# Fourteen products of ones, read by nothing, ahead of the first products of a graph network kernel

## What is computed

```
h = relu(layernorm(x))
for each of three layers:
    p   = relu(h @ Wp.T + bp)
    agg = segment_sum(p[src], dst) / max(count(dst), 1)
    h   = agg @ Wl.T + bl + h @ Wr.T
    after the first and the second layer: h = layernorm(relu(h)) * g + be
out = x + h
```

## Time and profile before

| | us |
|---|---|
| median of three runs | 1517.86 (1517.79 to 1518.0) |
| profiled execution, its own time | 1517.14 |
| span of that execution, first to last instruction | 1515.0 |
| PE busy in it | 1492.6 (99%) |
| DVE, ACT, POOL busy | 981.2, 687.1, 578.6 |

### The profile page before, as it was taken

One profiled execution on the slowest core, in us unless ns is written; L12 is line 12 of the kernel. 1 busy time (PEld: TensorE's weight loads), 2 busy tenths in 40 slices (PEclk: granted clock), 3 DMA queues, 4 the chain that ended last, 5 costly groups with the idle time before them and its releaser, 6 DMA issues.

```text
span 1515.0 us, 21400 instructions
## 1 busy us (share of the span) xinstructions
PE 1492.6 (99%) x7295; PEld 1221.5 (81%) x7295; DVE 981.2 (65%) x2164; ACT 687.1 (45%) x1267; POOL 578.6 (38%) x534
## 2 busy tenths in 40 slices
PE   7999999999999999999999999999999999999997
PEld 5787887888888888888888888888888888888886
DVE  7999975655555687777565655557766666555552
ACT  5545452232233577767322323357676652322322
POOL 4737754344323100100434442323354366444323
PEclk9999999999999999999999999999999999999999
DMA  8897877555554878887645555489999986455434
GB/s 301 319 377 249 271 249 238 111 90 89 93 85 56 242 263 306 271 275 253 216 108 90 88 93 88 54 244 320 345 329 324 328 292 207 80 89 90 73 45 60
DMA packets 152855, 291.72 MB, mean 193 GB/s; under 512 B 19885, under 2 KB 19948, under 8 KB 152620
## 3 DMA queue, kind: packets, MB, share of 16 engines
q1 hardware_dynamic: 123708, 224.81, 43.3%
q0 software_dynamic: 28464, 64.51, 24.7%
q10 hardware_dynamic: 576, 1.05, 0.2%
HBM read 132.33 MB, written 157.92 MB: 192 GB/s over the span
## 4 chain that ended last, share of the span: by engine, by line
PE 89%; DMA 4%; DVE 3%; issue 2%; POOL 1%; ACT 1%; SPq 0%; POOLq 0%; ACTq 0%; DVEq 0%
PE bank L737 12%; PE bank L736 12%; PE bank L738 12%; PE bank L724 9%; PE bank L820 7%; PE bank L822 7%; PE bank L821 7%; PE bank L841 7%; PE bank L843 7%; PE bank L842 7%; DMA node_x<-xn 2%; DVE stats L1073 1%; DVE rows_out L1103 1%; DVE h_low L1047 1%; DMA rows_in<-node_x,sorted_src 1%
## 5 line engine op out<-in xcount | busy, mean ns | idle before, releaser
L736 PE MATMUL bank<-w_high,h_low 128*128 128x512 f32 x900 | 374.6, 416 | 0.0
L737 PE MATMUL bank<-w_low,h_high 128*128 128x512 f32 x900 | 356.3, 396 | 0.0
L738 PE MATMUL bank<-w_high,h_high 128*128 128x512 f32 x900 | 354.5, 394 | 0.0
L981 ACT ACTIVATE h_high<-h_pre 128x500 fp32r<-128x500 f32 x120 | 74.6, 622 | 449.0 <-DVE h_pre L1284 449.0
L594 POOL DMA_INDIRECT rows_in<-node_x,sorted_src x120 | 124.1, 1034 | 274.6 <-PE bank L724 199.8
L927 ACT ACTIVATE h_high<-bank 128x512 fp32r<-128x512 f32 x221 | 131.4, 595 | 155.2 <-PE bank L724 155.0
L738 PEld LDWEIGHTS bank<-w_high,h_high 128*128 128x128 f32 x900 | 169.3, 188 | 40.3
L1050 DVE TENSOR_TENSOR h_low<-bank,h_high 128x512 fp32r<-128x512 f32 x152 | 105.0, 692 | 146.4 <-ACT h_high L927 144.5
L961 ACT ACTIVATE xn<-rows_in,off,rstd 128x512 f32<-128x512 f32 x237 | 189.4, 806 | 13.6 <-issue 9.0
L820 PE MATMUL bank<-xt_low,w_high 128*128 128x500 f32 x480 | 194.5, 405 | 0.0
L736 PEld LDWEIGHTS bank<-w_high,h_low 128*128 128x128 f32 x900 | 169.8, 189 | 30.3
(11 more groups left out here) (127 smaller groups left out, 2209.1 us busy)
## 6 DMA issues: line engine op xcount, KB each, us to landing
node_x<-xn SPq DMA_DIRECT2D x237, 256.0 KB, 3.9
rows_in<-node_z SPq DMA_DIRECT2D x158, 256.0 KB, 4.4
node_z<-rows_out SPq DMA_DIRECT2D x142, 256.0 KB, 2.8
out<-rows_out SPq DMA_DIRECT2D x79, 256.0 KB, 3.5
rows_in<-x SPq DMA_DIRECT2D x78, 256.0 KB, 4.6
residual<-x SPq DMA_DIRECT2D x78, 256.0 KB, 4.3
node_z<-bias_z SPq DMA_DIRECT2D x16, 256.0 KB, 3.6
rows_in<-node_x SPq DMA_DIRECT2D x16, 256.0 KB, 2.6
```

The lines of the kernel that those rows point to most:

```text
L736: nc.tensor.matmul(psum, low[:, k, :], w_high("r", l)[:, k, :], start=(k == 0), stop=False)
L737: nc.tensor.matmul(psum, high[:, k, :], w_low("r", l)[:, k, :], start=False, stop=False)
L738: last = nc.tensor.matmul(psum, high[:, k, :], w_high("r", l)[:, k, :], start=False, stop=(k == K - 1))
```

## The change

PE gets a function `keep_busy(count)`, which makes `count` products of `ones` by `ones` into the first 128 columns of bank 7. Nothing reads them, and they signal nothing. Bank 7 is written next by the product of tile 3, whose first instruction overwrites it. Twelve stand ahead of everything, behind a new wait for `ones_done`; two stand behind the turn of tile 0, ahead of the turn of tile 1.

```diff
+WARM = 12
+WARM_BETWEEN = 2
...
         @block.tensor
         def _(pe):
+            def keep_busy(count):
+
+                for _ in range(count):
+                    nc.tensor.matmul(bank[7][:, 0:P], ones[:], ones[:], start=True, stop=True)
+
+            pe.wait_ge(ones_done, 1)
+            keep_busy(WARM)
             pe.wait_ge(ident_done, 1)
...
                         node_product(l, i)
                     if is_product(l, i + AHEAD_TURN):
                         node_turn(l, i + AHEAD_TURN)
+                    if (l, i) == (0, -AHEAD_TURN):
+                        keep_busy(WARM_BETWEEN)
```

## The result

| | before | after |
|---|---|---|
| median of the timed runs of both, us | 1518.01 (1515.39 to 1519.72) | 1520.58 (1518.86 to 1522.97) |
| ratio | | 1.0018 [1.0011, 1.0025] |
| profiled execution, its own time | 1517.14 | 1519.67 |
| span of that execution | 1515.0 | 1517.6 |

The change makes the kernel slower by about 2.6 us, 0.18%. Forecast was 1515.9 us, 1.9 us faster, with 1518.0 as the upper end. The times of before spread over 4.3 us here, where the three runs that the forecast started from lay within 0.2 us.

The account below looks back on a forecast made before the run. PE, busy 99% of the span, was taken to set the end; 0.26 + 1.67 = 1.93 us off the profiled 1517.14 gives 1515.2, and with the kept 0.7 us 1515.9 us, range 1514.8 to 1518.0.

Parts of the forecast that it names:

- the upper end: Whole kernel: top of the forecast range, 1518.0 us, set to take in the plain case of no gain.
- The ones in the wait: Start of PE: twelve products from 1.1 us end 1.3 us or more ahead of the first turn at 7.59, costing nothing.
- The shorter of the two bounds: Twelve products at the start: done near 5.5 us if the clock comes up after 3.6 us.
- the longer bound: Twelve products at the start: all 24 halves at the low level, 5.1 us, done near 6.2 us.
- the first rival: Start of PE: ones don't raise the clock, or it falls before tile 0's product; no gain, 1517.9, or 1518.5; 15%.
- the 1.93 us: Start of PE: gain at the third turn, 0.26 us from an earlier first product plus 1.67 from its higher clock.
- The tightest place: The turn at 50.74 us, 0.35 us behind its rows after ACT's store wait; that margin was expected to hold.
- the second rival: The DMA takes the gain back: stores up to 48 us end unchanged, leaving 0.35 us, 1517.5; 6%.
- The rest of PE's waits: PE near 120 and 247 us: 3.0 us of waits hang on PE's own steps and move along.
- the outlasting of the first wait: Start of PE: ones take 13.0 us, first turn 6.5 us late; 1524.4, or 1522.4 with all the gain; 3%.
- a clock that comes up later: First product of tile 0: three more products at the low level, 3 x 0.20 us, 1518.5; within a rival of 15%.
- The distance of the timed runs to the profiled one: Whole kernel: the timed median is 0.7 us above the profiled 1517.14, a distance kept to reach 1515.9 us.

Follow-up runs that it names:

- again_after: The changed kernel, unchanged, run again for a second profile; 1520.82 us, ratio to before 1.0018.
- given_back: The changed kernel plus seven products of ones behind the product of tile 0, to take the lead away; 1521.76 us, ratio to before 1.0021.
- more_ones_both: The changed kernel with fourteen and three ones, zeros at step 45 (was 20), sorted list at 59 (was 61); 1512.41 us, ratio to before 0.9961.
- after_sorted_early: The changed kernel with the sorted list, and so the load of `carry`, at step 59 in place of 61; 1517.04 us, ratio to before 0.9994.
- one_column_2: Repeat of the changed kernel with each product of ones cut from 128 columns to one; 1527.49 us, ratio to before 1.0007.
- more_ones: The changed kernel with fourteen and three products of ones in place of twelve and two; 1526.16 us, ratio to before 0.9996.
- no_between: The changed kernel without the two products of ones between the turns; 1521.57 us, ratio to before 1.0019.
- ones_last: The kernel before with the fourteen products of ones at the end of PE's program; 1518.17 us, ratio to before 0.9999.
- one_column_more: The changed kernel with products of ones of one column, 22 ahead in place of twelve; 1531.21 us, ratio to before 1.0026.
- before_clear_late: The kernel before with the stores of zeros at step 45 in place of 20; 1524.37 us, ratio to before 0.9984.

## Why the prediction was wrong, point by point

- **The ones in the wait.** Right as far as PE's time goes. 24 halves from 1.08 to 5.54 us; the first turn at 7.64 (7.59 before). The shorter of the two bounds held, with the clock up in the last part of them; in `again_after` and `given_back` they lasted 5.49 us, to 6.57, past the longer bound and still 1.0 us ahead of the turn. That they "cost nothing" is another matter, see below.
- **The clock when it counts (the first rival).** Half right. In after it fell behind the ones and came back within the first product, in place of nine slow instructions one was slow. That cost 0.4 of the 1.93 us. In `again_after`, the same kernel, and in `more_ones_both`, where it stayed up, the third turn came at 13.44 and 13.45 us, with 13.44 forecast. The fourth turn of the kernels with twelve and two stands between 15.45 and 16.74 us, against 17.35: the gain is a matter of the execution, from 0.6 to 1.9 us. The Trainium skill, page "TensorE: Matmul & The Clock Gate", says in Part 1 that idleness brings the lower clock back and in Part 4 that a transpose doesn't count as activity in the same way. The rows of after agree so far as the fall to 0.50 at 7.7 us came behind 2.1 us of idle time and the level stayed low through the two turns; `again_after`, `given_back` and `after_sorted_early`, in which it held over the same turns, show that the turns alone don't decide.
- **The tightest place, 50.74 us (the second rival).** Right that it would hold, nearly: the turn came at 49.57, 0.35 us of the lead was lost by then.
- **"The rest of PE's waits (3.0 us near 120 and 247 us) hang on work that PE's own steps release, and move along."** This is the step that failed, together with "cost nothing" for the ones: the sum has one term, the 1.93 us, and none for what the ones do to these later waits. The waits do move along with PE: between `one_column_2` and `more_ones` 1.96 us of lead pass them and 1.8 arrive at the last product. But they don't stay what they were. With the ones at the start and the zeros and the sorted list where they were, lead or none, PE waits 1.85 to 1.93 us for DVE at the lookup in place of 0.86 to 0.98 in the two profiles of before, the load of `carry` takes 8.8 to 9.1 us in place of 7.3 to 7.7, and the way from the fourth turn to the second gathered turn is 2.5 to 4.8 us longer. In after it is 235.89 us in place of 231.67: 4.2 us lost, against 1.5 us of lead, is the +2.70 us. The rows for asking were in hand: the wait at 116 us hangs on DVE, DVE on ACT, ACT on the stores of `xn`, and these on 2 MB of zeros in a DMA that was already full at 1.05; the one at 247 us hangs on the load of `carry`. Neither chain was followed.
- **That what can't move would cost nothing more than the lead.** The second rival's price was a lead lost but for 0.35 us, 1517.5, and the upper end, 1518.0, was put at no gain at all, so that the time would at worst be that of before. In after two things go beyond: the clock fell behind the lookup, 1.6 us for seven products and a turn, and the load of `carry` took 1.8 us longer. The fall isn't needed for the loss, as `no_between` has none there. Of the rivals the outlasting of the first wait and a clock that comes up later were the only ones priced as a loss, and neither was what happened.
- **The distance of the timed runs to the profiled one.** The 0.7 us, from three runs within 0.2 us, was no measure of anything: 16 runs of before spread over 4.3 us. A gain of 1.9 us needed more runs than that to be seen at all.

What is shown: in the sets in which before takes 1518 to 1519 us the loss is not the lead (`given_back`, `no_between`), not the number of instructions (`ones_last`), and is undone by the sorted list two steps earlier (before and after then both stand at 1517). The zeros late give before 2.1 us and after 2.6 us, in different sets; in the profiles they undo what the ones lose up to the lookup (97.5 us from the fourth turn without ones, 97.0 with), but by the ratios after is still 0.15% behind before with them (0.9999 and 0.9984). With both moves the gain comes through to the end, in the profiles and in the times of one set. What is not shown, and so the cause of the loss stays open, is why the wait at the lookup is longer, and why the load of `carry` takes 8.8 to 9.1 us, in every profile with the additional instructions at the start and the sorted list at step 61 (for the wait, with the zeros at step 20 as well), and 7.3 to 7.7 us in those without. Two DMA queues of the profile are of the kind "instruction", and instructions at the start of PE's program shift the times of their packets. DMA queues of before from 95 to 106 us:

```profile
q8 instruction: 1, 0.02, 0.5%
q14 instruction: 1, 0.01, 0.2%
```

These two packets are absent from after in that stretch, where one such packet falls between 84 and 95 us. The one of q8 falls between 90 and 95 us in all fourteen profiles with additional instructions at the start, and between 100 and 105 us in all six without. That a shift happens is so read. That it lengthens the wait or the load is not shown by any run: the kernels with both moves have the same shift and lose nothing, it isn't plain how 0.5% of the engines' time would do it, and while the load of `carry` is under way neither before nor after has such a packet. It stays open as well why after was level with before in the last set.

## What to carry to other kernels

Before a gain at the start is carried to the end, go through every wait that the bounding engine has later, and follow each down to its last link: where that is a full DMA or one big transfer, don't take its length for given, as it can grow by more than the gain. Give a change back on purpose, as `given_back` does: if the loss stays with the lead gone, it isn't the lead that costs. Here two numbers moved were worth 4.7 us, and the ones 1.4 us once that was done. A change worth 0.1% wants ten or more runs of both kernels before anything is believed.

## What the runs showed of the hardware that I had not expected

- The granted clock fell in the middle of the kernel behind a single wait of 1.93 us: 0.50 from 116.9 to 120.3 us in after, at a cost of 1.6 us, with PE at work all the while. Of the eight profiles with a wait of 1.93 us at this lookup it fell in three (after, `again_after`, `one_column_more`) and stayed at 1.00 in five. Such stretches stand in kernels without ones too: `before_clear_late` has one from 261.0 to 264.4 us.
- A float32 product of one column costs 0.22 us a half at the low level, the same as one of 128 columns, and 24 of them left the clock down until 13.3 us, where 24 halves of 128 columns brought it up before they ended at 5.54 us in after.
- A load of 1249.8 KB took from 6.8 to 9.1 us from issue to landing, with the load itself the same and only other parts of the program changed. A gather that needed a store issued 3 to 4 us behind the load started only 2.2 to 2.5 us after the load had landed, 6.5 to 7.9 us behind the store; where the store was issued behind the landing, it started 3.2 us behind the store.
